# Eviction as one VectorE operation with x added in place, and the output bias added to x by GpSimd

## The chip, the cores and the metric

The kernel runs on one core of a Trainium2 chip. The metric is the device time of one execution in microseconds (us); lower is better. The engines are named TensorE (PE in the profile, its weight loads PEld), VectorE (DVE), ScalarE (ACT) and GpSimd (POOL); SyncE (SP) only issues transfers here.

## What is computed

The input x has 32 images of 512 channels and 56 x 56 = 3136 positions. Each image is group-normalised (32 groups of 16 channels), sent through a 1x1 convolution whose 512 x 512 weight is mixed for that image out of four weights, scaled and biased, and added to x:

```python
def _L0_conv_ref(x, ...):
    pooled = jnp.mean(x, axis=(2, 3))
    h = relu((pooled @ fc_w.T - abn_m) * (abn_g / jnp.sqrt(abn_v + EPS)) + abn_b)
    ch_att = jax.nn.sigmoid(h @ ch_w.T + ch_b)
    fl_att = jax.nn.sigmoid(h @ fl_w.T + fl_b)
    kn_att = jax.nn.softmax(h @ kn_w.T + kn_b, axis=1)
    agg_w = jnp.einsum('bk,koc->boc', kn_att, weight)
    xm = x * ch_att[:, :, None, None]
    y = jnp.einsum('bchw,boc->bohw', xm, agg_w)
    y = y * fl_att[:, :, None, None]
    inv = bn_g / jnp.sqrt(bn_v + EPS)
    return (y - bn_m[...]) * inv[...] + bn_b[...]

x = x + _L0_conv_ref(_gn(x), ...)      # _gn: group norm, 32 groups
```

## The kernel before

Work goes by chunks. A chunk is 448 positions of one image with all 512 channels, as four tiles of 128 channels; seven chunks make an image, and a ring of 14 chunk slots (`x_ring`, in the code `xs`) holds two images. The bodies of the engines are written out for 14 chunks s = 0 to 13 (a turn, two images) and looped 16 times. A chunk's number within its image is n = s % 7, and t = 0 to 3 counts the four output tiles of a chunk. Below, (3, 0) means n = 3, t = 0. Every engine runs its own list in order, and semaphores are the only links between them; there is no scheduler.

For each chunk f:

- SyncE loads it into its slot, and VectorE takes `bn_stats` of its four tiles (`stats`, placed by the table `stats_at`).
- ScalarE normalises it in four operations (`norm`, L227, two chunks ahead of the products) into one of two buffers `x_norm`, and copies it as 16-bit high halves `x_hi` (`split`, L236, one chunk ahead).
- VectorE subtracts to get the low halves `x_lo` (`split`, L357, one operation for the chunk).
- TensorE makes four products (`product`, L679 to L681), one for each output tile, of 12 matmuls each: high by high, low by high, high by low, over four input tiles. They go through seven PSUM banks in turn. The first product of a chunk waits for `lo_ready`, and each waits until its bank is emptied (`evac_done`).
- ScalarE empties a bank (`evacuate`, L245): times `out_scale`, plus `out_bias`, into the buffer `y`. VectorE adds two tiles of `y` to x in the ring slot (`add`, L363), and SyncE writes the slot out and loads the chunk 14 further on into it.

While the chunks of one image are multiplied, the weight of the next image b is prepared at fixed places (n, t): `channel_means` (2, 0) and `group_spread` (2, 1) on VectorE, with small TensorE products for the group means (L640) after the products of (2, 1), the group variances (L644) after (2, 3) and `hidden` (L649) after (3, 2). VectorE has `group_var` at (3, 0), `norms` at (3, 1), `logits` at (3, 3), `attentions` at (4, 1), three `mix_kernel` operations over the whole weight (L465) at (4, 2), (5, 0) and (5, 1), and four `split_weight` operations (L477) at (5, 3) and (6, 0). `norms` is a chain in which each operation waits for the one before. It starts from a guess that ScalarE makes (`guess`, at (3, 0), L251 and L253) and ends in `fc_pooled` (L411), for which TensorE's `hidden` product waits. TensorE's list has the fourth product of chunk n = 3 behind `hidden`, so it can't go on while `hidden` waits.

## Time and profile before

| | |
|---|---|
| median of 3 runs | 2114.44 us (2112.9 to 2115.34) |
| the profiled execution, first to last instruction | 2112.4 us |
| TensorE busy | 2056.3 us, 97% |
| VectorE busy | 1867.6 us, 88% |
| ScalarE busy | 1729.7 us, 82% |
| GpSimd busy | 0.2 us |

The profile shows one execution. Its own time is its span of 2112.4 us; no other time of that execution is given, and the runs shown lie 0.5 to 2.9 us above it, the median 2.0 us. Busy time is the union of an engine's records: an operation's duration (mean ns) includes a tail that overlaps the next operation, so the distance from start to start is shorter than the duration where operations follow one another.

### The profile page before, as it was taken

The page shows a single profiled execution, that of the slowest core. Times are in us where ns is not written, and L with a number is a line of the kernel's source. Part 1 is how long each engine was busy: PE and PEld are TensorE (multiplying, and loading weights), DVE is VectorE, ACT ScalarE, POOL GpSimd, SP SyncE. Part 2 cuts the span into 40 slices and gives each one's busy share as a digit, 9 for nine tenths or more (in the row PEclk, how much of TensorE's full clock was granted, in tenths as well). Part 3 has the DMA queues.
Part 4 walks back from the last instruction along what each step waited for, and adds up shares of the span by engine and source line. Part 5 has one row for each costly group of instructions (what it writes and reads, how often), then busy time and mean ns, then how long its engine had stood idle before and what let it go on. Part 6 is the DMA issues. An engine that isn't in the chain of part 4 may idle for free.

```text
span 2112.4 us, 33140 instructions
## 1 busy us (share of the span) xinstructions
PE 2056.3 (97%) x10948; PEld 1078.1 (51%) x10948; DVE 1867.6 (88%) x2886; ACT 1729.7 (82%) x2295; POOL 0.2 (0%) x4
## 2 busy tenths in 40 slices
PE   1999999999999999999999999999999999999998
PEld 0455555555555555555555555555555555555554
DVE  7889889889889899889899898898898998898973
ACT  4788888888888888888888888888888888888885
POOL 0000000000000000000000000000000000000000
PEclk9999999999999999999999999999999999999999
DMA  8465556565556565556655565665565655566522
GB/s 332 139 209 194 204 189 206 200 208 203 195 193 208 195 206 202 196 191 208 208 200 200 191 208 193 208 208 191 191 208 202 206 200 192 195 205 207 175 105 105
DMA packets 237284, 415.99 MB, mean 197 GB/s; under 512 B 7248, under 2 KB 236624, under 8 KB 236752
## 3 DMA queue, kind: packets, MB, share of 16 engines
q1 hardware_dynamic: 237264, 415.74, 57.6%
q8 instruction: 11, 0.18, 0.0%
q14 instruction: 9, 0.07, 0.0%
HBM read 210.19 MB, written 205.52 MB: 197 GB/s over the span
## 4 chain that ended last, share of the span: by engine, by line
PE 97%; DVE 1%; DMA 1%; ACT 1%; SPq 0%; issue 0%; DVEq 0%
PE product L679 32%; PE product L680 32%; PE product L681 32%; DMA x_ring<-x 1%; DVE mixed_weight L529 0%; DVE chunk_stats L349 0%; PE small L649 0%; SPq L193 0%; DVE w_lo L545 0%; PE small L640 0%; ACT y L290 0%; PE small L644 0%; ACT x_norm L227 0%; DVE x_lo L357 0%; ACT x_hi L236 0%
## 5 line engine op out<-in xcount | busy, mean ns | idle before, releaser
L679 PE MATMUL product<-x_hi,w_hi 128*128 128x448 f16 x3584 | 1264.5, 353 | 6.7 <-DVE x_lo L357 3.7
L680 PE MATMUL product<-x_lo,w_hi 128*128 128x448 f16 x3584 | 1264.6, 353 | 0.0
L681 PE MATMUL product<-x_hi,w_lo 128*128 128x448 f16 x3584 | 1264.4, 353 | 0.0
L245 ACT ACTIVATE y<-product,out_bias,out_scale 128x448 f32<-128x448 f32 x896 | 641.8, 716 | 275.2 <-PE product L681 270.5
L227 ACT ACTIVATE x_norm<-x_ring,norm_bias,norm_scale 128x448 f32<-128x448 f32 x896 | 671.1, 750 | 1.3 <-DVE norm_bias L409 1.3
L363 DVE TENSOR_TENSOR x_ring<-x_ring,y 128x896 f32<-128x896 f32 x448 | 481.5, 1087 | 100.0 <-ACT y L245 95.7
L679 PEld LDWEIGHTS product<-x_hi,w_hi 128*128 128x128 f16 x3584 | 356.1, 99 | 327.3 <-issue 5.1
L681 PEld LDWEIGHTS product<-x_hi,w_lo 128*128 128x128 f16 x3584 | 350.9, 98 | 328.2 <-issue 1.6
L680 PEld LDWEIGHTS product<-x_lo,w_hi 128*128 128x128 f16 x3584 | 350.8, 98 | 319.5 <-issue 1.3
L349 DVE BATCH_NORM_STATS2 chunk_stats<-x_ring 128x6 f32<-128x448 f32 x896 | 493.4, 616 | 1.3 <-DMA x_ring<-x 1.2
L357 DVE TENSOR_TENSOR x_lo<-x_norm,x_hi 128x1792 f16<-128x1792 f32 x224 | 452.4, 2019 | 19.7 <-ACT x_hi L236 19.7
L236 ACT ACTIVATE x_hi<-x_norm 128x1792 f16<-128x1792 f32 x224 | 380.2, 1697 | 7.1
L465 DVE SCALAR_TENSOR_TENSOR mixed_weight<-weight,kernel_att,mixed_weight 128x2048 f32<-128x2048 f32 x93 | 218.3, 2347 | 0.0
L271 ACT ACTIVATE w_hi<-mixed_weight,channel_att_scaled 128x512 f16<-128x512 f32 x124 | 79.4, 710 | 52.0 <-DVE mixed_weight L465 52.0
L477 DVE SCALAR_TENSOR_TENSOR w_lo<-mixed_weight,channel_att_scaled,w_hi 128x512 f16<-128x512 f32 x124 | 87.4, 747 | 0.0
L367 DVE TENSOR_TENSOR newton<-rstd_guess 128x4 f32<-128x4 f32 x32 | 5.2, 163 | 87.1 <-ACT rstd_guess L253 87.1
L265 ACT ACTIVATE mixed_weight<-weight,kernel_att 128x2048 f32<-128x2048 f32 x32 | 64.1, 2002 | 8.2 <-DVE kernel_att L449 8.2
L640 PE MATMUL small<-mean_var,params 128*128 128x4 f32 x64 | 9.3, 215 | 24.4 <-DVE mean_var L383 24.4
L383 DVE BATCH_NORM_AGGREGATE mean_var<-chunk_stats 128x2 f32<-128x42 f32 x128 | 30.3, 299 | 0.0
L640 PEld LDWEIGHTS small<-mean_var,params 128*128 128x128 f32 x64 | 12.3, 194 | 27.2 <-issue 24.4
L251 ACT ACTIVATE ln_var<-var_eps 128x4 f32<-128x4 f32 x32 | 6.2, 193 | 23.0 <-DVE var_eps L399 23.0
L426 DVE SCALAR_TENSOR_TENSOR head_products<-hidden,params 128x384 f32<-128x384 f32 x32 | 17.9, 558 | 1.1
(66 smaller groups left out, 261.5 us busy)
## 6 DMA issues: line engine op xcount, KB each, us to landing
x_ring<-x SPq DMA_DIRECT2D x224, 896.0 KB, 4.8
out<-x_ring SPq DMA_DIRECT2D x224, 896.0 KB, 3.9
weight<-wt SPq DMA_DIRECT2D x4, 1024.0 KB, 15.1
params<-par SPq DMA_DIRECT2D x1, 462.0 KB, 3.4
```

Source lines behind the costliest of these rows:

```text
L227: ins = nc.scalar.activation(xn[:, f % 2, t], xs[:, f % RING, t], ACT.Identity, bias=nbias[:, u, t:t + 1], scale=nscale[:, u, t:t + 1])
L236: nc.scalar.activation(xhi[:, f % 2], xn[:, f % 2], ACT.Copy).then_inc(hi_ready, 1)
L245: nc.scalar.activation(y[:, s % 2, t], acc[k % BANKS][:, 0:COLS], ACT.Identity, bias=obias[:, t:t + 1], scale=oscale[:, u, t:t + 1]).then_ ...
L271: nc.scalar.activation(whi[:, b % 2, t], mix[:, t], ACT.Copy, scale=catt[:, t:t + 1]).then_inc(whi_ready, 1)
L349: ins = nc.vector.bn_stats(bst[:, f // CHUNKS % 2, t, f % CHUNKS], xs[:, f % RING, t])
L357: nc.vector.tensor_tensor(xlo[:, f % 2], xn[:, f % 2], xhi[:, f % 2], ALU.subtract).then_inc(lo_ready, 1)
L363: nc.vector.tensor_tensor(xs[:, s, two], xs[:, s, two], y[:, s % 2, two], ALU.add).then_inc(add_done, 1)
L465: ins = nc.vector.scalar_tensor_tensor(out=mix[:, :, :], in0=w[:, k], scalar=katt[:, k:k + 1], in1=mix[:, :, :], op0=ALU.mult, op1=ALU.add)
L477: ins = nc.vector.scalar_tensor_tensor(out=wlo[:, b % 2, t], in0=mix[:, t], scalar=catt[:, t:t + 1], in1=whi[:, b % 2, t], op0=ALU.mult, o ...
L679: nc.tensor.matmul(bank, whi[:, u, t, cols], hi, start=(t == 0), stop=False)
L680: nc.tensor.matmul(bank, whi[:, u, t, cols], lo, start=False, stop=False)
L681: ins = nc.tensor.matmul(bank, wlo[:, u, t, cols], hi, start=False, stop=(t == CT - 1))
```

## The change

ScalarE's `evacuate` and VectorE's `add` are gone, and so are the buffer `y` and the semaphore `add_done`. A new `evacuate` on VectorE, one operation for each tile (896 in all), reads the bank, multiplies by `out_scale` and adds x from the ring slot, in place. GpSimd, which had no work, gets a list: for each chunk, when its norm on ScalarE is done (`xn_ready`), four `tensor_scalar` operations add `out_bias` to x in the ring slot, in place (`add_bias`). VectorE's evictions wait for them (`biased`). ScalarE's `split` waits for `mm_done` itself, since the eviction in front of it is gone. On VectorE `split`, which stood behind `norms` and `attentions` at t = 1, now stands ahead of them, and `channel_means`, `group_var` and the other preparing steps of a place stand ahead of that place's eviction. SyncE waits for the four evictions of a chunk in place of its two adds. Outside these lines only semaphore starts, a scratch buffer for the abs sums, and the wait of the first split change.

```diff
@@ -162,7 +160,9 @@
         first_mix_ready = sem("first_mix_ready")
         wlo_ready = sem("wlo_ready")
         lo_ready = sem("lo_ready")
-        add_done = sem("add_done")
+        obias_ready = sem("obias_ready")
+        biased = sem("biased")
+        bias_begun = sem("bias_begun")
 
         ln_ready = sem("ln_ready")
         guess_ready = sem("guess_ready")
@@ -204,7 +204,7 @@
                 for s in range(RING):
                     n = s % CHUNKS
                     b = 2 * i + s // CHUNKS
-                    sp.wait_ge(add_done, turn.at(2 * RING, 4 + 2 * (s + 1)))
+                    sp.wait_ge(evac_done, turn.at(4 * RING, BANKS + 4 * (s + 1)))
                     sp.dma_start(out_d[b, :, :, n * COLS:(n + 1) * COLS], xs[:, s]).then_inc(chunk_out[s], 16)
                     if not last:
                         sp.wait_ge(chunk_out[s], turn.at(16, 16))
@@ -229,21 +229,13 @@
                 if t == CT - 1:
                     ins.then_inc(xn_ready, 1)
 
-            def split(turn, f):
+            def split(turn, f, first=False):
 
 
                 act.wait_ge(xn_ready, turn.at(RING, f + 1))
+                if not first:
+                    act.wait_ge(mm_done, turn.at(4 * RING, 4 * f))
                 nc.scalar.activation(xhi[:, f % 2], xn[:, f % 2], ACT.Copy).then_inc(hi_ready, 1)
-
-            def evacuate(turn, s, t):
-
-                k = 4 * s + t
-                u = s // CHUNKS
-                act.wait_ge(mm_done, turn.at(4 * RING, k + 1))
-                if t % 2 == 0:
-                    act.wait_ge(add_done, turn.at(2 * RING, 2 * s + t // 2 + 1))
-                nc.scalar.activation(y[:, s % 2, t], acc[k % BANKS][:, 0:COLS], ACT.Identity,
-                                     bias=obias[:, t:t + 1], scale=oscale[:, u, t:t + 1]).then_inc(evac_done, 1)
 
             def guess(turn, b):
 
@@ -311,7 +302,6 @@
                     for t in range(CT):
                         if t == 0 and not (last and s + SPLIT_AHEAD >= RING):
                             split(turn, s + SPLIT_AHEAD)
-                        evacuate(turn, s, t)
                         if not (last and s + NORM_AHEAD >= RING):
                             norm(turn, s + NORM_AHEAD, t)
                         if prepare:
@@ -356,11 +346,14 @@
                 dve.wait_ge(hi_ready, turn.at(RING, f + 1))
                 nc.vector.tensor_tensor(xlo[:, f % 2], xn[:, f % 2], xhi[:, f % 2], ALU.subtract).then_inc(lo_ready, 1)
 
-            def add(turn, s, half):
-
-                dve.wait_ge(evac_done, turn.at(4 * RING, BANKS + 4 * s + 2 * half + 2))
-                two = slice(2 * half, 2 * half + 2)
-                nc.vector.tensor_tensor(xs[:, s, two], xs[:, s, two], y[:, s % 2, two], ALU.add).then_inc(add_done, 1)
+            def evacuate(turn, s, t):
+
+                k = 4 * s + t
+                dve.wait_ge(mm_done, turn.at(4 * RING, 4 + k + 1))
+                dve.wait_ge(biased, turn.at(4 * RING, k + 1))
+                nc.vector.scalar_tensor_tensor(out=xs[:, s, t], in0=acc[k % BANKS][:, 0:COLS],
+                                               scalar=oscale[:, s // CHUNKS, t:t + 1], in1=xs[:, s, t],
+                                               op0=ALU.mult, op1=ALU.add).then_inc(evac_done, 1)
 
             def newton(turn, r, guess_, v, t):
 
@@ -595,10 +588,8 @@
                     n, b = s % CHUNKS, s // CHUNKS + 1
                     prepare = not (last and b == 2)
                     for t in range(CT):
-                        if t == 0 and s:
-                            if prepare and n == 2:
-                                stats_complete(turn, b)
-                            add(turn, s - 1, 1)
+                        if t == 1 and not (last and s + SPLIT_AHEAD >= RING):
+                            split(turn, s + SPLIT_AHEAD)
                         for f, tile in stats_at(s, t):
                             if not (last and f >= RING):
                                 stats(turn, f, tile)
@@ -607,10 +598,6 @@
                         if prepare and (n, t) == (4, 1):
                             attentions(turn, b)
                             step(scaled_attentions(turn, b))
-                        if t == 1 and not (last and s + SPLIT_AHEAD >= RING):
-                            split(turn, s + SPLIT_AHEAD)
-                        if t == 2:
-                            add(turn, s, 0)
                         if prepare:
                             if (n, t) == (2, 0):
                                 channel_means(turn, b)
@@ -625,13 +612,39 @@
                             if (n, t) in ((5, 3), (6, 0)):
                                 for j in {3: (0, 1), 0: (2, 3)}[t]:
                                     split_weight(turn, b, j)
+                        if prepare and (n, t) == (1, 3):
+                            stats_complete(turn, b)
+                        evacuate(turn, s, t)
                     if s == CHUNKS - 1:
                         assert done[0] - before == STEPS, done[0] - before
-                add(turn, RING - 1, 1)
             with dve.Fori(0, TURNS - 1) as i:
                 body(i, False)
             body(TURNS - 1, True)
 
+        @block.gpsimd
+        def _(pool):
+            def add_bias(turn, f):
+
+
+                pool.wait_ge(xn_ready, turn.at(RING, f + 1))
+                pool.sem_inc(bias_begun, 1)
+                for t in range(CT):
+                    nc.gpsimd.tensor_scalar(xs[:, f % RING, t], xs[:, f % RING, t], obias[:, t:t + 1], None,
+                                            ALU.add).then_inc(biased, 1)
+
+            start = Turn(pool, 0)
+            pool.wait_ge(obias_ready, 1)
+            add_bias(start, 0)
+
+            def body(i, last):
+                turn = Turn(pool, i)
+                for s in range(RING):
+                    if not (last and s + SPLIT_AHEAD >= RING):
+                        add_bias(turn, s + SPLIT_AHEAD)
+            with pool.Fori(0, TURNS - 1) as i:
+                body(i, False)
+            body(TURNS - 1, True)
+
         @block.tensor
         def _(pe):
             def group_mean(turn, b):
```

The first place is VectorE's list around (3, 0) and (3, 1), the norms of the next image. Before, in the kernel's own line numbers (L363 is `add`, L399 `group_var`, L367 the first operation of the chain, L411 its last, L357 `split`; REGISTER_ALU rows prepare a wait's number):

```order
L363 TENSOR_TENSOR x_ring<-x_ring,y 128x896
L399 TENSOR_SCALAR var_eps<-small 128x4
L404 REGISTER_ALU
L367 TENSOR_TENSOR newton<-rstd_guess 128x4
...
L411 TENSOR_TENSOR fc_pooled<-params,pooled 128x128
L356 REGISTER_ALU
L357 TENSOR_TENSOR x_lo<-x_norm,x_hi 128x1792
L361 REGISTER_ALU
L363 TENSOR_TENSOR x_ring<-x_ring,y 128x896
```

The same place now (L354 is the new eviction, whose bank is the number behind `product`, L392 `group_var`, L347 `split`, L360 the first operation of the chain, L404 its last):

```order
L392 TENSOR_SCALAR var_eps<-small 128x4
L352 REGISTER_ALU
L354 SCALAR_TENSOR_TENSOR x_ring<-product_5,out_scale,x_ring 128x448
L346 REGISTER_ALU
L347 TENSOR_TENSOR x_lo<-x_norm,x_hi 128x1792
L397 REGISTER_ALU
L360 TENSOR_TENSOR newton<-rstd_guess 128x4
...
L404 TENSOR_TENSOR fc_pooled<-params,pooled 128x128
L352 REGISTER_ALU
L354 SCALAR_TENSOR_TENSOR x_ring<-product_6,out_scale,x_ring 128x448
```

Between `group_var` and the chain now stand the eviction of product (3, 0), which can't start before that product is done, and the low halves of a whole chunk.

The second place is ScalarE's list in the same chunk. Before (L236 is `split`, L245 `evacuate`, L227 `norm`, L251 and L253 the guess):

```order
L236 ACTIVATE x_hi<-x_norm 128x1792
L242 REGISTER_ALU
L244 REGISTER_ALU
L245 ACTIVATE y<-product_5,out_bias,out_scale 128x448
L227 ACTIVATE x_norm<-x_ring,norm_bias,norm_scale 128x448
L250 REGISTER_ALU
L251 ACTIVATE ln_var<-var_eps 128x4
L252 REGISTER_ALU
L253 ACTIVATE rstd_guess<-ln_var 128x4
L242 REGISTER_ALU
L245 ACTIVATE y<-product_6,out_bias,out_scale 128x448
L227 ACTIVATE x_norm<-x_ring,norm_bias,norm_scale 128x448
```

And now (L238 is `split`, L243 and L245 are the guess):

```order
L238 ACTIVATE x_hi<-x_norm 128x1792
L227 ACTIVATE x_norm<-x_ring,norm_bias,norm_scale 128x448
L242 REGISTER_ALU
L243 ACTIVATE ln_var<-var_eps 128x4
L244 REGISTER_ALU
L245 ACTIVATE rstd_guess<-ln_var 128x4
L227 ACTIVATE x_norm<-x_ring,norm_bias,norm_scale 128x448 x3
```

No operation of ScalarE in this chunk waits for a product of this chunk any more: the split, the guess and all four norms can follow one another from the chunk's start. GpSimd's list behind them is, for every chunk alike, the wait for the norms and four operations of this kind:

```order
L629 REGISTER_ALU
L632 TENSOR_SCALAR x_ring<-x_ring,out_bias 128x448 x4
L629 REGISTER_ALU
L632 TENSOR_SCALAR x_ring<-x_ring,out_bias 128x448 x4
L629 REGISTER_ALU
```

## Rows read from the trace of the kernel before

**Rows 1.** The page: busy time of each engine, and the granted clock by slice

```profile
PE 2056.3 (97%) x10948; PEld 1078.1 (51%) x10948; DVE 1867.6 (88%) x2886; ACT 1729.7 (82%) x2295; POOL 0.2 (0%) x4
PEclk9999999999999999999999999999999999999999
```

**Rows 2.** Who waited for whom: us in total, times, longest us

```profile
DVE newton L367 <- ACT rstd_guess L253: 87.1, 31, 2.8
PE product L679 <- DVE x_lo L357: 3.7, 1, 3.7
```

**Rows 3.** Groups of instructions: shapes, count, busy us, mean ns, idle before

```profile
L227 ACT ACTIVATE x_norm<-x_ring,norm_bias,norm_scale 128x448 f32<-128x448 f32 x896 | 671.1, 750 | 1.3 <-DVE norm_bias L409 1.3
L349 DVE BATCH_NORM_STATS2 chunk_stats<-x_ring 128x6 f32<-128x448 f32 x896 | 493.4, 616 | 1.3 <-DMA x_ring<-x 1.2
L363 DVE TENSOR_TENSOR x_ring<-x_ring,y 128x896 f32<-128x896 f32 x448 | 481.5, 1087 | 100.0 <-ACT y L245 95.7
L465 DVE SCALAR_TENSOR_TENSOR mixed_weight<-weight,kernel_att,mixed_weight 128x2048 f32<-128x2048 f32 x93 | 218.3, 2347 | 0.0
L477 DVE SCALAR_TENSOR_TENSOR w_lo<-mixed_weight,channel_att_scaled,w_hi 128x512 f16<-128x512 f32 x124 | 87.4, 747 | 0.0
L741 POOL MEMSET const-float32-1.0<- 128x1 f32 x1 | 0.1, 98 | 0.0
```

**Rows 4.** VectorE in order of time: start us, length us, count (1010 to 1054)

```profile
1010.49 1.41 DVE L477 SCALAR_TENSOR_TENSOR w_lo<-mixed_weight,channel_att_scaled,w_hi 128x512 f16<-128x512 f32 x2
...
1046.95 0.16 DVE L399 TENSOR_SCALAR var_eps<-small 128x4 f32<-128x4 f32 x1
1049.91 0.16 DVE L367 TENSOR_TENSOR newton<-rstd_guess 128x4 f32<-128x4 f32 x1 [2.81 <-ACT rstd_guess L253]
...
1051.05 0.28 DVE L411 TENSOR_TENSOR fc_pooled<-params,pooled 128x128 f32<-128x128 f32 x1
1051.25 2.02 DVE L357 TENSOR_TENSOR x_lo<-x_norm,x_hi 128x1792 f16<-128x1792 f32 x1
1053.19 1.08 DVE L363 TENSOR_TENSOR x_ring<-x_ring,y 128x896 f32<-128x896 f32 x1
```

**Rows 5.** TensorE in order of time: the small products around chunk 3

```profile
1044.98 0.28 PE L644 MATMUL small<-spread,params 128*128 128x4 f32 x2
...
1051.93 0.38 PE L649 MATMUL small<-fc_pooled,ones 128*128 128x128 f32 x2
```

**Rows 6.** ScalarE in order of time, the same chunk

```profile
1046.59 1.70 ACT L236 ACTIVATE x_hi<-x_norm 128x1792 f16<-128x1792 f32 x1
1048.19 0.71 ACT L245 ACTIVATE y<-product,out_bias,out_scale 128x448 f32<-128x448 f32 x1
1048.80 0.75 ACT L227 ACTIVATE x_norm<-x_ring,norm_bias,norm_scale 128x448 f32<-128x448 f32 x1
1049.45 0.19 ACT L251 ACTIVATE ln_var<-var_eps 128x4 f32<-128x4 f32 x1
...
1049.86 0.72 ACT L245 ACTIVATE y<-product,out_bias,out_scale 128x448 f32<-128x448 f32 x1
...
1052.21 0.72 ACT L245 ACTIVATE y<-product,out_bias,out_scale 128x448 f32<-128x448 f32 x1 [0.98 <-PE product L681]
```

**Rows 7.** All engines in order of time: the start

```profile
43.87 2.70 ACT L227 ACTIVATE x_norm<-x_ring,norm_bias,norm_scale 128x448 f32<-128x448 f32 x4
...
46.61 0.13 DVE L567 TENSOR_SCALAR weight_unscale<-weight_top_all 128x1 f32<-128x1 f32 x1
...
47.97 2.30 DVE L545 SCALAR_TENSOR_TENSOR w_lo<-mixed_weight,channel_att_scaled,w_hi 128x128 f16<-128x128 f32 x8 [0.57 <-ACT w_hi L303]
...
58.05 4.30 DVE L349 BATCH_NORM_STATS2 chunk_stats<-x_ring 128x6 f32<-128x448 f32 x8
```

**Rows 8.** All engines in order of time: the end

```profile
2106.24 0.72 ACT L245 ACTIVATE y<-product,out_bias,out_scale 128x448 f32<-128x448 f32 x1 [1.55 <-PE product L681]
2106.99 1.09 DVE L363 TENSOR_TENSOR x_ring<-x_ring,y 128x896 f32<-128x896 f32 x1 [3.45 <-ACT y L245]
```

More of the change, by code:

```diff
@@ L83, in build @@
         xlo = sb("x_lo", [P, 2, CT, COLS], f16)
-        y = sb("y", [P, 2, CT, COLS])
+        scratch = sb("abs_scratch", [P, CT * C])
         w = sb("weight", [P, KERNELS, CT, C])
@@ L134, in build @@
         top_row, top_all = small[0:1, 64:64 + P], small[:, 200:201]
-        y_free = y[:, :, :, :].rearrange("p a t n -> p (a t n)")[:, 0:CT * C]
         def p_(name):
@@ L274, in _ @@
             act.preload_act_table_set("natural_log_exp_and_others")
-            act.sem_inc(evac_done, BANKS)
             start = Turn(act, 0)
@@ L283, in _ @@
                 norm(start, 0, t)
-            split(start, 0)
+            split(start, 0, True)
             for k in range(KERNELS):
@@ L289, in _ @@
                     act.wait_ge(abs_done, k)
-                nc.scalar.activation(y_free, w[:, k], ACT.Abs, accum_out=wsum[:, k:k + 1]).then_inc(abs_done, 1)
+                nc.scalar.activation(scratch[:, :].rearrange("p (t n) -> p t n", t=CT), w[:, k], ACT.Abs, accum_out=wsum[:, k:k + 1]).then_inc(abs_done, 1)
                 if k == 0:
@@ L485, in _ @@
             start = Turn(dve, 0)
-            dve.sem_inc(add_done, 4)
+            dve.sem_inc(evac_done, BANKS)
             nc.vector.memset(ones[:, :], 1.0).then_inc(const_ready, 1)
@@ L497, in _ @@
             after(start)
-            step(nc.vector.tensor_tensor(obias[:, :], p_("bn_b"), obias[:, :], ALU.subtract))
+            nc.vector.tensor_tensor(obias[:, :], p_("bn_b"), obias[:, :], ALU.subtract).then_inc(obias_ready, 1)
             for f in range(CHUNKS):
@@ L652, in _ @@
             start = Turn(pe, 0)
+            pe.sem_inc(mm_done, 4)
             pe.wait_ge(params_in, 16)
```

## Prediction

> **What bounds the kernel now.** I first read the page's busy times and clock [rows 1]. The reader sees TensorE busy for 97% of the span at the full granted clock, in 10948 records that advance at 2056.3 / 10948 = 0.188 us each, so a product of 12 matmuls takes 2.25 us and a chunk of four 9.0 us. VectorE is at 88%, ScalarE at 82%, GpSimd does nothing. Then the waits, to see whether TensorE is ever kept waiting after the start: the only wait of its products of any size is one of 3.7 us [rows 2], at the second chunk. So TensorE's stream sets the time, and the waits of VectorE (95.7 us for evictions [rows 3], 87.1 us for the guess, 31 times [rows 2]) cost nothing by themselves. A faster eviction can give nothing in the middle. What the change can do is to delay something that TensorE waits for. So the question for each edit is the slack to TensorE, and I went through an image chunk by chunk in the three engines' order of time [rows 4 to 6].
>
> **The change part by part.** Times here are on the clock of the stretch shown, so that they can be laid beside the rows.
>
> *The new eviction, its length.* No row has it. The nearest is VectorE's scalar_tensor_tensor with 512 columns: 0.75 us long [rows 3], and two in a row take 1.41 [rows 4], so the second starts 1.41 - 0.75 = 0.66 after the first. VectorE's columns cost (2.02 - 1.09) / 896 = 0.00104 us each, by the 1792- and the 896-column operations [rows 3, 4], so 64 fewer give 0.66 - 0.07 = 0.59. Whether reading a bank costs more no row of VectorE of that size shows; ScalarE's read of a bank is no longer than its read of x_ring (0.72 against 0.75 [rows 6]). I take 0.60, with 0.75 as upper bound, the whole duration of the 512-column one.
>
> *VectorE's load.* Per image it has 1867.6 / 32 = 58.4 us. The adds take away 481.5 / 32 = 15.0 and 28 evictions bring 28 x 0.60 = 16.8: 60.2 us, against 28 x 2.25 = 63.0 us for TensorE. At 0.75 it would be 64.4, a little over. I take 60.2: VectorE stays under TensorE, but with 3 us to spare per image instead of 5. Chunks 4 and 5 of an image hold the three mixings of 2.35 us [rows 3]: chunk 4 has statistics of four tiles 2.2, low halves 1.9, small steps about 0.9 (an estimate, eight or so of 0.16 as in [rows 4], partly overlapped), a mixing 2.35 and four evictions 2.4, together 9.8 us; chunk 5 has two mixings 4.7, low halves 1.9, two `w_lo` 1.3 and evictions 2.4, together 10.3. Against 9.0 that is a lag of 2 us. The low halves of a chunk may start about 4.2 us after the first product of the chunk before is done (three products, 6.75, less the eviction and split, 2.5), so that lag is hidden.
>
> *The place of the norms.* This is what decides. `hidden` was issued at 1051.93 [rows 5]; between the variance product at 1044.98 and it lie three products (6.75 us). Before, the chain of `norms` ran from 1049.91 to 1051.33 [rows 4], 1.42 us, 0.6 ahead of it. Now the eviction of (3, 0) and the low halves stand in front of the chain. ScalarE had waited for product (3, 2) until 1052.21 [rows 6], so product (3, 0) was to be had at 1052.21 - 2 x 2.25 = 1047.7. Eviction 0.60: 1048.3. Low halves 1.94 (1051.25 to 1053.19 [rows 4]): 1050.25. Chain 1.42: 1051.67. That is 0.26 us ahead of 1051.93, and it repeats for each of 31 images [rows 2]: a slack of a quarter microsecond in a place where TensorE has the fourth product behind its wait. By itself it costs nothing; with a 0.75 eviction it has 0.1 left.
>
> *GpSimd's bias.* Chunk 3 begins at about 1052.21 - 3 x 2.25 - 0.2 = 1045.3. ScalarE has nothing of that chunk to wait for: high halves 1.60 (1046.59 to 1048.19), a norm 0.65 (1048.80 to 1049.45), the guess 0.41 (to 1049.86) [rows 6], three norms 0.65 + 0.65 + 0.75. `xn_ready` comes at 1045.3 + 4.7 = 1050.0, and GpSimd's four operations start there, beside the low halves' end and then beside the chain (1050.25 to 1051.67). What one of them takes, no row shows. The only GpSimd rows are 0.10 us memsets of one column, a lower bound with no columns in it; passes over the same 448 columns take 0.62 us on VectorE and 0.75 on ScalarE [rows 3]. I take 0.7, that is 2.8 for the four. The upper bound that matters is 2.25, where GpSimd would itself need a product's time for each tile.
>
> *What the two do to each other.* Both work on the same SBUF, and the trace of before can't say whether they disturb each other, since GpSimd was idle. The bounds are nothing, and each of the four GpSimd operations coming once between two steps of the chain, which has eight steps with gaps: 2.8 us. I take the upper one. The slack of 0.26 is small beside either engine's operations, the chain is short steps that each give the other side an opening, and a short step pays a whole GpSimd operation each time. The cost is then 2.8 - 0.26 = 2.5 us per image, 31 x 2.5 = 79 us.
>
> The Trainium skill, "SBUF — State Buffer", section "SBUF: two separate sides", says that VectorE and GpSimd have one pair of ports in common, an exclusive lock held for a whole instruction, which a VectorE operation with two SBUF inputs and a GpSimd operation that reads SBUF fight over. By it the sum would be that of the exclusion, 79 us, and without it 0; no row of before shows it. The "GPSIMD Engine Reference", section "Elementwise — side-by-side cycle accounting", gives some 1.8 cycles for an element in the best case, and for our 448 columns an estimate of 0.67 us; by it the four would take 2.7 us.
>
> *Other places where they meet.* The first mixing waits for ScalarE's part, which starts later than before since the low halves now go ahead of `attentions`; mixings, low halves and `w_lo` of chunks 4 to 6 meet GpSimd too. Adding 0.7 us for up to four meetings uses up the lag allowance there; I take 0 and keep 1 us per image, 31 us, for the range. *Start*: the norms of chunk 1 end at 46.57 [rows 7], GpSimd's four then lie beside the steps from 46.61 and the first `w_lo`, which TensorE waits for: up to 2.8 us. In the first chunk the eviction (0, 0) also stands between the eight statistics and the low halves for which TensorE waited 3.7 us: 0.6. *End*: ScalarE's last eviction and VectorE's add took 2106.24 to 2108.08 [rows 8], 1.84; one eviction of 0.68 in their place gains 1.2. SyncE's waits and ScalarE's lost evictions touch nothing that TensorE waits for.
>
> *Sum* on the profile's span: 2112.4 + 79 + 2.8 + 0.6 - 1.2 = 2193.6 us. The runs' median is 2.0 us above the span: 2196 us, or 3.9% slower.
>
> **The rivals.** A measurement of this kernel tells 0.2%, or 4.2 us, from no change.
>
> *No disturbance, nothing slower.* If the engines don't exclude each other, the 0.26 us holds and the chain is on time: 2114.4 - 1.2 + 0.6 = 2114 us. For it: every load above fits. Against it: it needs every term in a 4 us path right to 6%. If the eviction is 0.75 and its two waits cost 0.2 more, 0.1 us per image is missing, 3 us, so it decides at 0.26 us of extra delay. Chance 0.15. With up to 0.3 us per image missing, to 2123 us: 0.07.
>
> *Disturbed in part.* GpSimd starts late, or only one or two of its four come in between: 1.4 - 0.26 = 1.1 us per image, 36 us, 2152 us. Chance 0.17.
>
> *The forecast*, 2.0 to 3.3 us per image: 2177 to 2220 us. Chance 0.38.
>
> *A slower GpSimd operation.* At 1.2 us each the four take 4.8: 31 x 4.5 = 141 us, and the places of chunks 4 to 6 add their 31: 2230 to 2290 us. Chance 0.13. From 2.25 us on GpSimd is the bound; at 2.5, 28 of them are 70 us per image against 63, and 2114 x 70 / 63 = 2350 us. Chance 0.07.
>
> *Faster.* The middle has nothing to give, so only the end's 1.2 us and a start without meetings: 2112 us, with VectorE free of two-tile adds at a good moment perhaps less. It would need over 4.2 us from 50 us of start. Chance 0.03.
>
> **How the numbers follow.** The predicted time is the forecast's, 2196 us. The range runs from 2112, the lower edge of the undisturbed case, to 2260, the middle of the slow-operation case; outside lie the GpSimd bound, half of the 0.13 and little of the faster case, some 0.15. The forecast's own range is 2177 to 2220. Faster 0.03, same 0.15, slower 0.82 (0.07 + 0.17 + 0.38 + 0.13 + 0.07).
>
> **What would show it.** In the new profile: TensorE's `hidden` product waits for `fc_pooled` some 2.5 us, 31 times, and TensorE's busy share falls to 93 or 94%. The chain from its first step to `fc_pooled` is 4 us long instead of 1.42, with GpSimd's operations between its steps. The eviction is near 0.67 us long and GpSimd's operation starts every 0.7 us. The prediction is wrong if the chain keeps its 1.42 us beside GpSimd, if GpSimd's four are over before the low halves end, or if TensorE waits mostly at another place, as for `x_lo` or for a bank.

## The result and the profile after

The changed kernel takes 2143.62 us (median of 4 runs, 2143.36 to 2145.04) against 2114.89 us before (4 runs): ratio 1.0139, 95% interval 1.0125 to 1.0153. It is slower, as forecast, but by 29 us and not by 82. Both profiled spans tell the same: 2141.7 us against 2112.4.

The page of the changed kernel, busy times, granted clock and the queue that brings instructions:

```profile
PE 2072.9 (97%) x10948; PEld 1071.9 (50%) x10948; DVE 1998.5 (93%) x3334; ACT 1135.2 (53%) x1399; POOL 1664.2 (78%) x900
...
PEclk9999999999999999999999999999999999999999
...
q14 instruction: 79, 0.65, 0.1%
```

VectorE has gone from 88 to 93% and ScalarE from 82 to 53% [rows 1], and GpSimd is busy for 78% of the span. The clock is full, so TensorE lost time by waiting. Its groups and the longest waits:

```profile
L632 POOL TENSOR_SCALAR x_ring<-x_ring,out_bias 128x448 f32<-128x448 f32 x896 | 1664.0, 1876 | 455.3 <-ACT x_norm L227 455.3
L354 DVE SCALAR_TENSOR_TENSOR x_ring<-product,out_scale,x_ring 128x448 f32<-128x448 f32 x896 | 584.8, 672 | 62.1 <-PE product L695 51.7 <-DVE chunk_stats L339 5.8 <-issue 4.4
L347 DVE TENSOR_TENSOR x_lo<-x_norm,x_hi 128x1792 f16<-128x1792 f32 x224 | 463.5, 2069 | 2.0
L458 DVE SCALAR_TENSOR_TENSOR mixed_weight<-weight,kernel_att,mixed_weight 128x2048 f32<-128x2048 f32 x93 | 218.2, 2346 | 41.9 <-ACT mixed_weight L257 41.9
L402 DVE SCALAR_TENSOR_TENSOR norm_bias<-group_mean,norm_scale 128x4 f32<-128x4 f32 x32 | 17.0, 530 | 1.8
```

```profile
DVE mixed_weight L458 <- ACT mixed_weight L257: 41.9, 31, 1.4
PEld product L693 <- issue: 37.1, 70, 4.6
PEld small L662 <- DVE fc_pooled L404: 25.5, 32, 3.6
```

The eviction is 0.672 us long. GpSimd's operation is 1.88 us on average, not 0.7. One small VectorE operation, `norm_bias`, is now 530 ns long (161 before); the mixing (L458) is as long as before [rows 3]. TensorE's weight load for `hidden` waits for `fc_pooled` 32 times. VectorE in order of time, one chain of the norms:

```profile
1063.28 0.68 DVE L354 SCALAR_TENSOR_TENSOR x_ring<-product,out_scale,x_ring 128x448 f32<-128x448 f32 x1 [0.44 <-PE product L695]
1063.88 2.02 DVE L347 TENSOR_TENSOR x_lo<-x_norm,x_hi 128x1792 f16<-128x1792 f32 x1
1065.81 0.16 DVE L360 TENSOR_TENSOR newton<-rstd_guess 128x4 f32<-128x4 f32 x1
1066.00 0.41 DVE L362 TENSOR_TENSOR newton<-newton,var_eps 128x4 f32<-128x4 f32 x1
...
1066.84 0.34 DVE L399 TENSOR_SCALAR norm_scale<-rstd 128x4 f32<-128x4 f32 x1
...
1067.25 0.54 DVE L402 SCALAR_TENSOR_TENSOR norm_bias<-group_mean,norm_scale 128x4 f32<-128x4 f32 x1
1067.71 0.28 DVE L404 TENSOR_TENSOR fc_pooled<-params,pooled 128x128 f32<-128x128 f32 x1
```

GpSimd, the same stretch (start, length of all, count):

```profile
1065.70 5.62 POOL L632 TENSOR_SCALAR x_ring<-x_ring,out_bias 128x448 f32<-128x448 f32 x4 [2.21 <-ACT x_norm L227]
```

TensorE, the same stretch and the start of chunk 6 of that image:

```profile
1067.43 0.35 PE L695 MATMUL product<-x_hi,w_lo 128*128 128x448 f16 x1
1068.05 0.49 PE L662 MATMUL small<-fc_pooled,ones 128*128 128x128 f32 x2 [0.27 <-DVE fc_pooled L404]
1068.37 0.35 PE L693 MATMUL product<-x_hi,w_hi 128*128 128x448 f16 x1
...
1088.61 0.35 PE L695 MATMUL product<-x_hi,w_lo 128*128 128x448 f16 x1
1089.08 0.36 PE L693 MATMUL product<-x_hi,w_hi 128*128 128x448 f16 x1
```

The reader is to see four things. The chain runs from 1065.81 to 1067.99, 2.18 us where it had 1.42 [rows 4]: some of its steps are 0.12 to 0.38 us longer, and GpSimd starts 0.11 us ahead of it. The two matmuls around `hidden` start 0.94 us apart; before it was 0.41, so TensorE loses 0.53 us there. At the start of chunk 6 the distance is 0.47 in place of 0.19, and VectorE's low halves of that chunk ended just before. And the "idle" given for `hidden`, 0.27, is less than what is lost: matmuls are shown longer than the distance at which they start, so losses are read from the distances of the starts. I summed them that way over the trace, beyond 0.19 us (beyond before's 0.41 around `hidden`): 16.4 us at `hidden` (31 times), 11.7 us at the first product of chunk 6 or of the next image's chunk 0 (45 times), and 1 us or so in the start. That is the loss, 29 us.

### The profile page after: what moved, and what is told of

Read it like the earlier page. It is cut to its first block, busy times and chain, and to the rows that moved or that the text cites. A ratio compares the mean times of both kernels' runs of the same rounds, so it can differ in the third digit from the quotient of the medians.

```text
span 2141.7 us, 34276 instructions
## 1 busy us (share of the span) xinstructions
PE 2072.9 (97%) x10948; PEld 1071.9 (50%) x10948; DVE 1998.5 (93%) x3334; ACT 1135.2 (53%) x1399; POOL 1664.2 (78%) x900
## 4 chain that ended last, share of the span: by engine, by line
PE 73%; DVE 16%; issue 5%; ACT 4%; DMA 1%; DVEq 0%; SPq 0%; ACTq 0%
PE product L693 24%; PE product L695 24%; PE product L694 24%; DVE x_lo L347 6%; DVE mixed_weight L458 3%; DVE chunk_stats L339 1%; DVE x_ring L354 1%; ACT mixed_weight L257 1%; ACT w_hi L263 1%; ACT x_hi L238 1%; DMA x_ring<-x 1%; DVE newton L362 1%; DVE head_products L419 0%; ACT x_norm L227 0%; PE small L662 0%
## 5 line engine op out<-in xcount | busy, mean ns | idle before, releaser
L632 POOL TENSOR_SCALAR x_ring<-x_ring,out_bias 128x448 f32<-128x448 f32 x896 | 1664.0, 1876 | 455.3 <-ACT x_norm L227 455.3
L238 ACT ACTIVATE x_hi<-x_norm 128x1792 f16<-128x1792 f32 x224 | 380.2, 1697 | 638.3 <-PE product L695 628.2
L354 DVE SCALAR_TENSOR_TENSOR x_ring<-product,out_scale,x_ring 128x448 f32<-128x448 f32 x896 | 584.8, 672 | 62.1 <-PE product L695 51.7
L227 ACT ACTIVATE x_norm<-x_ring,norm_bias,norm_scale 128x448 f32<-128x448 f32 x896 | 616.7, 746 | 2.5 <-DVE norm_bias L402 1.3
L347 DVE TENSOR_TENSOR x_lo<-x_norm,x_hi 128x1792 f16<-128x1792 f32 x224 | 463.5, 2069 | 2.0
L458 DVE SCALAR_TENSOR_TENSOR mixed_weight<-weight,kernel_att,mixed_weight 128x2048 f32<-128x2048 f32 x93 | 218.2, 2346 | 41.9 <-ACT mixed_weight L257 41.9
L419 DVE SCALAR_TENSOR_TENSOR head_products<-hidden,params 128x384 f32<-128x384 f32 x32 | 27.8, 869 | 1.1
L662 PE MATMUL small<-fc_pooled,ones 128*128 128x128 f32 x64 | 15.9, 331 | 11.8 <-DVE fc_pooled L404 11.8
L662 PEld LDWEIGHTS small<-fc_pooled,ones 128*128 128x128 f32 x64 | 9.7, 191 | 25.5 <-DVE fc_pooled L404 25.5
```

What stands on the lines that cost most here:

```text
L227: ins = nc.scalar.activation(xn[:, f % 2, t], xs[:, f % RING, t], ACT.Identity, bias=nbias[:, u, t:t + 1], scale=nscale[:, u, t:t + 1])
L238: nc.scalar.activation(xhi[:, f % 2], xn[:, f % 2], ACT.Copy).then_inc(hi_ready, 1)
L347: nc.vector.tensor_tensor(xlo[:, f % 2], xn[:, f % 2], xhi[:, f % 2], ALU.subtract).then_inc(lo_ready, 1)
L354: nc.vector.scalar_tensor_tensor(out=xs[:, s, t], in0=acc[k % BANKS][:, 0:COLS], scalar=oscale[:, s // CHUNKS, t:t + 1], in1=xs[:, s, t], ...
L458: ins = nc.vector.scalar_tensor_tensor(out=mix[:, :, :], in0=w[:, k], scalar=katt[:, k:k + 1], in1=mix[:, :, :], op0=ALU.mult, op1=ALU.add)
L632: nc.gpsimd.tensor_scalar(xs[:, f % RING, t], xs[:, f % RING, t], obias[:, t:t + 1], None, ALU.add).then_inc(biased, 1)
```

## The experiments

Each time is the median of the kernel's runs and the ratio is to the kernel before on the same chip. The last columns say where TensorE loses time, summed as above: at `hidden`; at the starts of chunk 6 and the next chunk 0; at the start of the second chunk of a turn. "Packets" are the instruction packets of queue q14, and "body" is the number of instructions in VectorE's loop, counted in the built program.

| kernel | us | ratio (95%) | hidden | chunks 6, 0 | turn's 2nd | packets | body |
|---|---|---|---|---|---|---|---|
| before | 2114.89 | 1 | 0 | 0 | 0 | 9 | 275 |
| changed | 2143.62 | 1.0139 (1.0125 to 1.0153) | 16.4 | 11.7 | 0 | 79 | 385 |
| e1 norms first | 2120.36 | 1.0026 (1.0016 to 1.0037) | 0 | 4.3 | 0 | 79 | 385 |
| e2 attentions first | 2146.41 | 1.0149 (1.0134 to 1.0165) | 16.5 | 0 | 15.3 | 79 | 385 |
| e3 both first | 2126.15 | 1.0054 (1.0040 to 1.0068) | 0 | 0 | 10.4 | 79 | 385 |
| e4 GpSimd after norms | 2125.18 | 1.0049 (1.0035 to 1.0063) | 0 | 8.9 | 0 | 79 | 385 |
| e5 no bias | 2116.21 | 1.0008 (0.9999 to 1.0017) | 0.1 | 1.6 | 0.3 | 79 | 385 |
| e6 half the columns | 2138.05 | 1.0111 (1.0096 to 1.0127) | 18.8 | 3.7 | 0 | 79 | 385 |
| e7 both first, one wait | 2121.66 | 1.0033 (1.0020 to 1.0045) | 0 | 0 | 5.7 | 79 | 343 |
| e8 before, 8 waits more | 2152.74 | 1.0180 (1.0166 to 1.0194) | 0 | 4.0 | 30.9 | 81 | 387 |
| e9 bias on ScalarE | 2117.04 | 1.0010 (1.0001 to 1.0019) | 0 | 0 | 1.6 | 79 | 329 |
| e11 before, 4 waits more | 2143.49 | 1.0134 (1.0119 to 1.0150) | 0 | 0 | 27.1 | 80 | 331 |
| e12 bias on ScalarE, pairs | 2114.23 | 0.9999 (0.9990 to 1.0008) | 0 | 0 | 0 | 8 | 304 |

e8 loses another 3.1 us at the start of the second image's chunk 5 (15 times), for which the table has no column. e10 isn't in the table; it is told with e9.

**e1, e2, e3: the order of VectorE's list.** The edit of e3; e1 does it for n = 3 alone and e2 for n = 4 alone:

```diff
-                        if t == 1 and not (last and s + SPLIT_AHEAD >= RING):
-                            split(turn, s + SPLIT_AHEAD)
                         for f, tile in stats_at(s, t):
...
                         if prepare and (n, t) == (4, 1):
                             attentions(turn, b)
                             step(scaled_attentions(turn, b))
+                        if t == 1 and not (last and s + SPLIT_AHEAD >= RING):
+                            split(turn, s + SPLIT_AHEAD)
```

> The changed kernel with one move undone: at (3, 1) the norms chain stands ahead of the low halves again. In the changed kernel TensorE loses 0.53 us at the hidden product in each of 31 images, 16.4 us. Theory (the chain stands too late behind the low halves): that goes, 2143.6 - 16.4 = 2127 us, and the gap before the product behind hidden is again 0.41 us. Rival (VectorE is simply short of time once GpSimd works beside it, and what is won here is lost at the next low halves): 2139 to 2144 us.

> The changed kernel with the other move undone: at (4, 1) the attentions stand ahead of the low halves. In the changed kernel TensorE waits for low halves 0.2 to 0.3 us at three chunk starts per turn (chunk 6 of one image, chunk 7 of both), some 12 us in all, and VectorE's first mixing waits 1.35 us for ScalarE's part, 31 times. Theory (the late attentions delay the three mixings, and these the low halves of chunks 6 and 7): the mixing's wait goes, and the time is 2143.6 - 12 = 2132 us. Rival (those waits come from VectorE's load, evictions and meetings with GpSimd): 2140 to 2144 us.

> Both moves undone: norms and attentions ahead of the low halves, eviction on VectorE and bias on GpSimd as in the changed kernel. Theory (the order costs everything, the move of the work nothing): 2143.6 - 28.4 = 2115 us, or 2113 to 2116. Rival (part of the loss is the work itself): 2120 us or more.

e1 gives back 23 us, more than the 16.4 at `hidden`: two thirds of the loss at chunks 6 and 0 goes as well; e4 to e6 tell why. e2 and e3 missed. With the attentions first the mixing no longer waits (0.0 us on L458) and chunks 6 and 0 start on time, but a loss of another kind appears. VectorE of e3 at a turn's start:

```profile
961.14 1.26 DVE L354 SCALAR_TENSOR_TENSOR x_ring<-product,out_scale,x_ring 128x448 f32<-128x448 f32 x2
964.75 2.21 DVE L339 BATCH_NORM_STATS2 chunk_stats<-x_ring 128x6 f32<-128x448 f32 x4 [2.35 <-issue]
966.87 0.67 DVE L354 SCALAR_TENSOR_TENSOR x_ring<-product,out_scale,x_ring 128x448 f32<-128x448 f32 x1
967.46 2.02 DVE L347 TENSOR_TENSOR x_lo<-x_norm,x_hi 128x1792 f16<-128x1792 f32 x1
```

The statistics there need nothing that isn't long in place; the engine stands still for its own instructions ("issue"), 32.4 us in 14 turns, and the low halves behind it are late by 0.74 us a turn.

**e4, e5, e6: GpSimd beside the chain.** The edits: e4 adds a wait for the norms to the bias of chunk 5 of an image, e5 leaves the bias out of the result and counts `biased` on by four in place of GpSimd's four operations (not in the code below), e6 adds it to half the columns alone.

```diff
                 pool.wait_ge(xn_ready, turn.at(RING, f + 1))
+                if gated:                       # e4, f % 7 == 5
+                    pool.wait_ge(norm_ready, turn.at(2, f // CHUNKS + 2))
...
-                    nc.gpsimd.tensor_scalar(xs[:, f % RING, t], xs[:, f % RING, t], obias[:, t:t + 1], None,
+                    nc.gpsimd.tensor_scalar(xs[:, f % RING, t, 0:COLS // 2], xs[:, f % RING, t, 0:COLS // 2], obias[:, t:t + 1], None,
```

> The changed kernel, its order kept, but GpSimd's four operations that fall beside the norms chain wait until the chain is done; no work is left out. Theory (GpSimd stretches the chain from 1.42 to 2.2 us, and only with that is it late): the chain is 1.42 us again, TensorE has no wait at hidden, 2143.6 - 16.4 = 2127 us. Rival (the order alone makes it late): the wait of about 0.5 us stays, 2143 us.

> The changed kernel without GpSimd's bias operations: the output bias is left out of the result, GpSimd only counts its semaphore on; VectorE's list is the same. Theory (the chain of the norms is late only because GpSimd's four operations beside it stretch it from 1.42 to 2.2 us): the chain is 1.42 us, nothing waits at hidden, and the low halves of chunks 6 and 7 still come late since the attentions stand late: 2143.6 - 16.4 = 2127 us or down to 2125 as with the gated GpSimd. Rival (GpSimd also costs at the mixings and low halves of chunks 4 to 6): all waits go, 2115 to 2118 us.

> The changed kernel with GpSimd adding the bias to 224 of 448 columns in each of its operations (the other half of the output lacks the bias). It tells what one GpSimd operation holds up. Theory A (VectorE is held for a short fixed time when a GpSimd operation starts or ends): the operation is about 0.8 us instead of 1.40, more of them fit beside the chain, which stays at 2.1 to 2.3 us or grows, and the time stays at 2140 to 2145 us. Theory B (the hold-up goes with the columns that GpSimd moves): the chain falls to about 1.8 us and the time to about 2132 us.

e4 leaves all the work and the order in place and moves four GpSimd operations by 1.5 us: the loss at `hidden` is gone, and the time is 18.4 us lower. But 8.9 of the 11.7 us at chunks 6 and 0 stay, with the chain on time. Without the bias (e5) nearly everything is gone, though the attentions still stand behind the low halves and the mixing still waits 41.8 us; that was the rival's outcome. VectorE of e5, the same chain:

```profile
988.06 0.16 DVE L360 TENSOR_TENSOR newton<-rstd_guess 128x4 f32<-128x4 f32 x1
988.25 0.17 DVE L362 TENSOR_TENSOR newton<-newton,var_eps 128x4 f32<-128x4 f32 x1
...
988.86 0.17 DVE L399 TENSOR_SCALAR norm_scale<-rstd 128x4 f32<-128x4 f32 x1
...
989.12 0.16 DVE L402 SCALAR_TENSOR_TENSOR norm_bias<-group_mean,norm_scale 128x4 f32<-128x4 f32 x1
989.20 0.28 DVE L404 TENSOR_TENSOR fc_pooled<-params,pooled 128x128 f32<-128x128 f32 x1
```

1.42 us again, and it ends at 989.48, ahead of `hidden` at 989.87. The first chain step, 988.06, follows product (3, 0) and the low halves exactly as in the changed kernel, so the order alone fits with 0.2 to 0.4 us to spare.

What is lost at chunks 6 and 0 comes in the main from a second meeting. The low halves of chunk 6 start 17.97 us after `hidden` in e5 (1007.84 - 989.87) and 18.54 in the changed kernel (1021.77 - 1003.23), where `hidden` is late itself. Of these 0.57 us, 0.32 arise in `logits`, the next chain of small steps: its step `head_products` (L419) takes 0.88 us in place of 0.56. The changed kernel, then e5:

```profile
1069.91 1.42 POOL L632 TENSOR_SCALAR x_ring<-x_ring,out_bias 128x448 f32<-128x448 f32 x1
1070.09 0.88 DVE L419 SCALAR_TENSOR_TENSOR head_products<-hidden,params 128x384 f32<-128x384 f32 x1
```

```profile
991.67 0.56 DVE L419 SCALAR_TENSOR_TENSOR head_products<-hidden,params 128x384 f32<-128x384 f32 x1
```

In e4 the four moved operations meet `logits` too, at its second step (shortest, median and longest, ns):

```profile
L413 DVE TENSOR_TENSOR hidden<-hidden,params x32: 193/556/559, 32.0 to 2026.0; 128x32 f32<-128x32 f32 x32
```

The loss at chunks 6 and 0 follows what `logits` grows by: 1.6 us where neither chain grows (e5), 3.7 where only that of the norms does (e6), 4.3 with a step 0.23 us longer (e1), 8.9 with 0.36 (e4), 11.7 in the changed kernel with 0.32 and the rest of the chain's delay. It takes the order as well: with the attentions ahead of the low halves (e2, e3) nothing is lost there.

e6 tells what kind of hold-up it is. GpSimd's and VectorE's rows of e6:

```profile
L632 POOL TENSOR_SCALAR x_ring<-x_ring,out_bias x896: 837/845/4728, 32.9 to 2110.4; 128x224 f32<-128x224 f32 x180
```

```profile
998.33 0.37 DVE L364 TENSOR_SCALAR newton<-newton 128x4 f32<-128x4 f32 x1
998.73 0.38 DVE L366 TENSOR_TENSOR rstd<-rstd_guess,newton 128x4 f32<-128x4 f32 x1
999.15 0.37 DVE L399 TENSOR_SCALAR norm_scale<-rstd 128x4 f32<-128x4 f32 x1
```

With GpSimd operations of 0.845 us in place of 1.403 the chain isn't shorter but 2.26 us long (997.88 to 1000.14), and now four steps are stretched by about 0.2: shorter operations disturb it more often. The chain's hold-up doesn't fall with GpSimd's columns, as theory A said, though a single one does: 0.22 us at most here, 0.38 in the changed kernel. The whole time fell by 5.6 us nevertheless, below theory A's range: GpSimd's four are over before `logits`, whose `head_products` keeps its 0.557 us, and only 3.7 us are lost at chunks 6 and 0.

The changed kernel's rows say where in a GpSimd operation VectorE is held:

```profile
1067.14 1.40 POOL L632 TENSOR_SCALAR x_ring<-x_ring,out_bias 128x448 f32<-128x448 f32 x1
1055.58 1.40 POOL L632 TENSOR_SCALAR x_ring<-x_ring,out_bias 128x448 f32<-128x448 f32 x1
1055.66 2.42 DVE L347 TENSOR_TENSOR x_lo<-x_norm,x_hi 128x1792 f16<-128x1792 f32 x1
```

`norm_bias`, from 1067.25, is 0.38 us longer than in e5, `head_products`, from 1070.09, 0.32, and these low halves, from 1055.66, 0.41. Taken from the starts of the GpSimd operations beside them (1067.14, 1069.91, 1055.58), all three delays end after 0.49 or 0.50 us. So it is the first half microsecond of a GpSimd operation that holds these up, and the rest of its 1.4 us doesn't. That doesn't account for every step: `norm_scale`, 0.17 longer, stands near a GpSimd operation's end.

**e7, e8, e11: the length of VectorE's loop.** e7 waits for the bias once per chunk; e8 and e11 put waits that are always satisfied into the kernel before.

```diff
-                dve.wait_ge(biased, turn.at(4 * RING, k + 1))
+                if t == 0:                                        # e7
+                    dve.wait_ge(biased, turn.at(4 * RING, k + 4))
...
             def add(turn, s, half):
+                for _ in range(8):                                # e8; e11: 4
+                    dve.wait_ge(const_ready, 2)
                 dve.wait_ge(evac_done, turn.at(4 * RING, BANKS + 4 * s + 2 * half + 2))
```

> The kernel with norms and attentions ahead of the low halves, whose VectorE now waits for GpSimd's bias once per chunk instead of before each eviction: VectorE's loop body has 343 instructions instead of 385 (before the change 275). Theory (VectorE's loop no longer stays in its instruction memory, so each turn starts with a fetch, the 2.35 us on issue at the first statistics of 14 turns, and TensorE waits 0.74 us for the second chunk's low halves): with the shorter body the instruction packets fall from 79 to 9, the wait goes, and the time is 2126.2 - 10.4 = 2116 us. Rival (the wait has to do with VectorE's load or the extra waits themselves, not with fetching, or 343 are still too many): 79 packets or 2124 to 2126 us.

> The kernel before with eight waits on an always satisfied constant ahead of each VectorE add, so that its loop body has 387 instructions instead of 275; no work or order is changed. Theory (a body of that length is fetched anew each turn and VectorE, which is on time, stands still for it): instruction packets go from 9 to 79, VectorE idles some 2.3 us on issue at each turn's start; the low halves of the second chunk stand after 4 statistics, 2.1 us, so they end some 0 to 0.8 us late, and the time is 2115 to 2126 us. Rival (length alone costs nothing): 9 packets, 2115 us.

> The kernel before with four satisfied waits ahead of each VectorE add in place of eight: 331 instructions in the loop body, 275 before, 387 with eight. It tells the waits' own cost from that of a body that is too long. Theory (a threshold between 331 and 343 instructions or above): 9 instruction packets, 2115 to 2117 us. If the threshold lies below: 79 or 81 packets, an idle of 2 to 3 us at each turn's start, 2125 to 2152 us. Rival (the 38 us of eight waits are the waits' own time on VectorE, whatever is fetched): about half of it, 2134 us, with 9 packets.

Waits that do nothing cost the kernel before 38 us (e8) and 29 us (e11), as much as the whole change. e8's forecast, 2126 us at most, missed. e11, its queue and its VectorE:

```profile
q14 instruction: 80, 0.66, 0.1%
```

```profile
DVE chunk_stats L349 <- issue: 40.1, 14, 3.2
PE product L681 <- DVE x_lo L357: 28.0, 15, 3.2
```

At each of 14 turns VectorE idles 2.9 us on issue, the low halves behind it come late, and TensorE loses 27.1 us. Half the waits left three quarters of the cost, so most of it isn't the waits' own time: the packets say what it is, 80 against 9. What e8 loses more, at chunks 0 and 5 and at the turn's second chunk, may be the waits' own time; no run tells. e7's body of 343 was still too long, and so was e11's of 331; there my threshold was wrong.

The Trainium skill, "Runtime: NRT & Kernel Launch", section "Instruction fetch mechanics", says that an engine holds two blocks of 256 instructions and that a branch to a place outside them waits for a transfer. The runs agree in kind: bodies of 275 and 304 stay, 329 and more are fetched anew. They don't agree in size. VectorE's start has 127 instructions in front of e9's loop; by an estimate from the page's blocks a loop of 329 would end at 456, within two of them if the first began with the start, and still it was fetched anew. No run moved the loop, so why the limit lies between 304 and 329 stays open.

**e9, e10, e12: the bias elsewhere.** e9 is e3 with the bias on ScalarE, behind each norm; the low halves that TensorE waits for are made after it, so VectorE needs no wait for it. e12 also puts the evictions in pairs behind one wait. e10 is e3 with GpSimd's bias waited for by TensorE, once per chunk.

```diff
+            def add_bias(f, t):                                   # e9, e12, in ScalarE's list
+                nc.scalar.activation(xs[:, f % RING, t], xs[:, f % RING, t], ACT.Identity, bias=obias[:, t:t + 1])
...
-                dve.wait_ge(mm_done, turn.at(4 * RING, 4 + k + 1))
-                dve.wait_ge(biased, turn.at(4 * RING, k + 1))
+                if t % 2 == 0:                                    # e12; e9 keeps the wait of each
+                    dve.wait_ge(mm_done, turn.at(4 * RING, 4 + k + 2))
...
+                    pe.wait_ge(biased, turn.at(4 * RING, 4 * s + 4))   # e10, ahead of a chunk's first product
```

> Norms and attentions ahead of the low halves, eviction on VectorE, and the bias added to x by ScalarE (which has the time since its evictions are gone) behind each of its norms; GpSimd does nothing and VectorE needs no wait for the bias, since the low halves that TensorE waits for are made after it: 329 instructions in VectorE's loop. Theory (only GpSimd beside VectorE, and the fetch of a loop body that is too long, cost anything): no wait of TensorE in the middle, the end 1.2 us shorter, 2113 to 2115 us. If 329 instructions are still too many: 79 instruction packets and 2119 to 2124 us. Rival (VectorE's load with 896 evictions costs by itself): TensorE waits for low halves or banks in chunks 5 to 7 of each image, 2118 us or more with 9 packets.

> Norms and attentions ahead of the low halves, bias on GpSimd; TensorE waits for the bias once per chunk in VectorE's place, so that VectorE's loop has 329 instructions instead of 385. Theory (what is left of the loss with both moves undone, 2126.2 us, is the fetch at each turn): with 9 instruction packets 2115 to 2117 us; if 329 are still too many, 79 packets, VectorE idles at the turn's start and the time stays at 2120 to 2126 us. Rival (GpSimd's work still costs with the order restored): 9 packets and 2120 us or more.

> As e9_scalar_bias (bias on ScalarE, norms and attentions first), but VectorE's evictions stand in pairs behind one wait for a product, at t = 1 and t = 3: 304 instructions in its loop instead of 329. Kernels with 329 to 385 instructions fetched anew at each turn (79 to 81 instruction packets), the one with 275 did not. Theory (the fetch is all that e9 has left over the bound): if 304 fit, 9 packets, no wait of VectorE at the turn's start, TensorE without a wait in the middle, and about 2113 us, 0.1% under the kernel before. If they don't: 79 packets and 2114 to 2117 us. Rival (pairs make VectorE late for low halves or banks): TensorE waits in chunks 4 to 7 of each image, 2118 us or more.

e10 took 2314.31 us (ratio 1.0938, 1.0924 to 1.0953) and tells nothing of its question: I had overlooked that GpSimd's operations, stretched to up to 4.7 us beside the mixings, are then on TensorE's path. Its waits:

```profile
PEld product L693 <- DVE x_ring L353: 135.9, 30, 4.5
PE product L693 <- POOL x_ring L631: 122.8, 30, 4.1
```

TensorE waited 123 us for GpSimd in 30 places, ahead of chunk 6 of an image. After such a wait of some 4 us the granted clock was 0.50, its lower level of 1.2 GHz, from 1246.5 to 1253 us of that trace, and 1.00 before and behind; the mean fell to 0.961.

e9 has all 896 evictions on VectorE and loses 1.6 us in TensorE's middle, all of it at the turn's start; it was forecast at 2119 us or more for 79 packets, and VectorE idles only 1.4 us a turn there. e12, page and queue:

```profile
PE 2057.4 (97%) x10948; PEld 1078.4 (51%) x10948; DVE 1944.6 (92%) x3334; ACT 1625.4 (77%) x2295; POOL 0.2 (0%) x4
```

```profile
q14 instruction: 8, 0.07, 0.0%
```

304 instructions fit, TensorE waits nowhere in the middle, and the time is that of the kernel before (0.9999). In this form the move of the evictions is free, and worth nothing: TensorE was and is the bound.

## Why the prediction was wrong

The place and the kind of disturbance were the ones forecast: TensorE's `hidden` waits for a chain that GpSimd stretches. What GpSimd does to that chain was wrong, 79 us forecast and 16.4 measured. That the whole is only three times too large, 82 us against 29, is luck in part: the forecast's GpSimd operation was too short, and another place, taken at nothing, gave 11.7 us.

- **What bounds the kernel.** Right: in e12 VectorE evicts everything and the time is that of before.
- **The eviction.** Right: 0.672 us long, two in a row 1.26, so 0.59 from start to start; forecast 0.60.
- **The place of the norms.** Right: the low halves before the chain leave a slack of 0.2 to 0.4 us (forecast 0.26), and e5 shows that it holds.
- **GpSimd's operation.** Wrong by a factor of two: 1.403 us undisturbed (the median), not 0.7. The rows for 448 columns of VectorE and ScalarE, 0.62 and 0.75, were no guide; with e6's 0.845 for 224 columns a GpSimd column costs 2.5 ns and an operation 0.29 us besides.
- **What the two do to each other.** This is the step that failed: "I take the upper one", 2.8 us for the four. The chain grew by 0.76 us. That "a short step pays a whole GpSimd operation each time" was not so: an operation of 1.4 us added 0.12 to 0.38 us to a step, and to four of the eight steps only. With the measured 1.40 the prediction's rule would give 31 x (5.6 - 0.26) = 166 us, ten times what was lost at `hidden`. Per image 0.76 - 0.26 = 0.5 us was to be expected of that at `hidden`, 31 x 0.5 = 15.5; measured 16.4.
- **Other places.** Taken at 0, measured 11.7 us. New meetings were allowed for in the range, but at the mixings, the low halves and `w_lo`; the one that counts is in `logits` (0.32 us per image), and with the rest of the chain's delay it comes through `attentions` and the mixings to the low halves of chunks 6 and 0. The order alone costs 1.6 us there (e5).
- **TensorE's busy share.** Forecast as 93 or 94%, measured 97%: matmuls are shown longer than the distance of their starts, so the share hardly moves.
- **The loop's length.** Not in the prediction at all. In the changed kernel it costs nothing that can be seen, since VectorE is behind TensorE there and no wait on issue stands at the turn's start (79 packets all the same). That being behind is what hides the fetch is argued from e1 and e3, not shown. The attentions ahead of the low halves uncover it (e2, e3, e7); the norms alone ahead (e1) do not.

The Trainium skill, "SBUF — State Buffer", section "SBUF: two separate sides", gives an exclusive lock for a whole instruction to whichever of the two engines starts first. The traces agree for one side: GpSimd's operation is 1.397 us at least and up to 4.73 beside mixings and low halves, and these mixings and low halves keep their own 2.35 and 2.0 us. For the other side they don't: with GpSimd first, a VectorE operation was held up 0.4 us at most, in the chain, in `logits` and once per image in low halves (2.42 us), never 1.4. The measurement decides.

The changed kernel's row for GpSimd (shortest, median and longest, ns):

```profile
L632 POOL TENSOR_SCALAR x_ring<-x_ring,out_bias x896: 1397/1403/4727, 32.7 to 2118.3; 128x448 f32<-128x448 f32 x180
```

## What to carry to other kernels

Where one engine sets the time, ask of a moved operation not what it costs but what then stands ahead of the next thing that engine waits for; a slack of 0.26 us in a chain that repeats 31 times was gone once a third engine worked beside it, and cost 16 us. Look at the next chain of small steps too: it brought most of the other 12, though nothing waited there. Put work on GpSimd away from chains of small VectorE steps, and don't let the bound engine wait for it beside long VectorE operations. Count the instructions of a loop body, waits and register steps too: look at the instruction queue's packets after each change.

## What the hardware showed that I had not expected

- A loop body that is fetched anew: 304 instructions 8 packets, 329 to 387 79 to 81 packets, and up to 2.9 us of VectorE per turn where nothing hides it.
- GpSimd's tensor_scalar on 448 float32 columns takes 1.40 us alone and up to 4.73 us beside VectorE's operations with two SBUF inputs that began before it. The mixing isn't lengthened, 2.346 us in both kernels; 29 of 224 low halves are, to 2.42 us, those that start 0.1 us or so behind a GpSimd operation.
- Small VectorE steps beside GpSimd grow by 0.1 to 0.4 us, and with GpSimd operations of 0.845 us by about 0.2 but more often. Several of these delays end 0.49 us after the start of a GpSimd operation of 448 columns.
